# Three small loads moved behind the first gates, first rows ahead of the first block sum, first feature block turned in two banks

## The chip, the cores and the metric

The kernel runs on one core of one Trainium2 chip. The metric is the device time of one execution in microseconds (us); lower is better. Before the change the median of three runs is 175.96 us (175.79 to 176.62).

## The reference, cut to what matters

All data is f32. `x` is 2 batches x 512 rows x 512 features.

```
mod = (silu(c) @ wmod).reshape(2, 6, 1, 512)         # c: 2 x 512, wmod: 512 x 3072
sa, ca, ga, sb, cb, gb = mod[:, 0], ..., mod[:, 5]
ga, gb = guarded: sign(g) * max(|g|, 0.25)
h = layernorm(x) * (1 + ca) + sa
x = x + ga * (h @ (weight * block_mask).T)           # 32x32 blocks kept where the mask has any 1
h = layernorm(x) * (1 + cb) + sb
gate, up = (h @ Wg.T) * ag, (h @ Wu.T) * au          # 1376 inner features, ternary weights
x = x + gb * (((silu(gate) * up) @ Wd.T) * ad)
```

## The kernel before

Rows are cut into tiles of 128 (`TT` = 4 tiles a batch), features into blocks of 128 (`KT` = 4). Five instruction streams are written out by hand, one for each engine, in the order in which they run; semaphores alone tie them together. No scheduler moves anything.

SyncE (SP) issues the big loads in one long queue: the four `x` tiles of batch 0, the first mask block, the first modulation weights (`mod_ln1` 0, semaphore `d_ln1[0]`), the first attention weights, more modulation weights and masks, the `x` tiles of batch 1, and so on. After the first half of `mod_ln2` it waits for the normalised rows of batch 1 (`xn_ok`), issues seven moves of 32-row blocks inside SBUF (`move_first`, L246), then the rest of `mod_ln2` and the second `mod_gate` (L298 to L301), and then the chunks of the FFN weights (L308, L309).

ScalarE (ACT) issues four small loads first: `cond` (L385), the per-feature scales `scal` (L386), `adc` (L387) and the tail of `scal` (L389). The last three share the semaphore `d_small`, which is waited for by the first SiLU of the FFN (L504), by the first product behind it on VectorE (L698), and by `guard_gate(1)`.

The opening works as follows. VectorE (DVE) takes the statistics of the four tiles of batch 0 (`stats`), sums the first mask block (`sum_mask(0)`, L603) and normalises the first 256 features of the four tiles (`normalise_half(0, ...)`, L556). TensorE (PE) runs 17 warm-up matmuls (L1074), then `mask_blocks(0)` (L869: spreads the mask's block sums), `rows_first` (L813: the first modulation rows), the transposes of feature block 0 (`transposes(0, ...)`, L885), `columns(0)` (L859: turns the modulation rows), the transposes of feature block 1, and the first of the 32 attention products (`linear`, L906; two matmul records each). Between the attention products stand more of these small steps, in the table `between`. DVE turns the block sums into a 0/1 mask (`keep_blocks`, L608) and the rows into modulation columns (`mod_columns`, L615). GpSimd (POOL) multiplies the attention weights with that mask (`mask_weights`, L352). ACT copies the rows (`copy_rows`, L402) and applies scale and shift to the turned rows (`modulate`, L427 for the part that is done on its own, L430 for the rest).

Later steps that the prediction speaks of: `mask_blocks(2)` on PE lets DVE run `keep_blocks(2)` and then `normalise(1)` (L576), whose end lets SP issue its moves; `rows_last` on PE (48 instructions of L813) waits for the second `mod_gate`; after it stand the rest of the attention products and then the FFN (L935 gate and up products, L1005 down products, 22 steps). ACT checks each FFN weight chunk with `check_chunk` (L442) when the chunk has landed.

Of the kernel before, what the change touches and what calls it, by code (L numbers as in the profile page):

```python
# [26 lines left out]
ACT = mybir.ActivationFunctionType  # L27
# [3 lines left out]
P = 128  # L31
# [3 lines left out]
TT = 4  # L35
SEQ = TT * P
# [19 lines left out]
MOVES = [(i, j) for i in range(P // BLK) for j in range(P // BLK) if i != j]  # L56
BY_SYNC = 7
LAG = 2
FIRST_ALONE = [0, 3]
HELD = 4  # L60
HALF = D // 2
SHIFT = BLK + NB
# [14 lines left out]
def adaln_block(nc, x, att_w, att_mask, cond, mod_ln1, mod_ln2, mod_gate, w_gu, w_gu_tail, w_down,  # L77
                scales, scales_tail, down_scale, out):
    with ExitStack() as ctx:
# [3 lines left out]
        def sem(name):  # L83
            return ctx.enter_context(nc.semaphore(name))
# [116 lines left out]
        rstd_ok = sem("rstd_ok")  # L201
        xn_ok = sem("xn_ok")
        xt_done = sem("xt_done")
        h_first = sem("h_first")
        h_ok = sem("h_ok")
        h_hi = sem("h_hi")
# [176 lines left out]
        @block.scalar  # L383
        def _(act):
            act.dma_start(condt[:, :, :], cond).then_inc(d_cond, 16)  # L385
            act.dma_start(scal[:, 0:C - 1, :], scales).then_inc(d_small, 16)  # L386
            act.dma_start(adc[:, :], down_scale).then_inc(d_small, 16)  # L387
            act.wait_ge(zeroed, 2)
            act.dma_start(scal[0:FT, C - 1, :], scales_tail).then_inc(d_small, 16)  # L389
            act.wait_ge(d_cond, 16)  # L390
            act.wait_ge(zeroed, 3)
            act.activation(sc[:, :, :].rearrange("p j (i m) -> p j i m", m=SHIFT)[:, :, :, 0:NB],
# [3 lines left out]
            def copy_rows(n):  # L396
                act.wait_ge(rows_done, n + 1)
                if n == 0:
                    act.wait_ge(consts_ok, 6)
                if n == 3:  # L400
                    act.wait_ge(cols_done, 1)
                act.activation(rows[:, n % 3, :], bank[2 if n == 3 else 6][:, 0:P], ACT.Identity,  # L402
                               bias=onerow[:, 0:1]).then_inc(rows_copied, 1)
# [7 lines left out]
            def modulate(n):  # L411

                q, k = divmod(n, KT)
                layer, b = divmod(q, NB)
                act.wait_ge(xt_done, n + 1)
                act.wait_ge(modc_ok, SETS if layer else SET_OF[k] + 1)
                if q < 2:
                    dst = h1[:, b, k, :]
                else:
                    dst = hbuf[:, n % 2, :]  # L420
                    if n >= 10:
                        act.wait_ge(h_lo, n - 9)
                src = [bank[4 + n % 2][:, :], xturn[:, k, :], bank[n % 2][:, :], xn[:, k, :]][q]
                part = slice(0, SEQ)
                if n in FIRST_ALONE:
                    part = slice(P, SEQ)
                    act.activation(dst[:, 0:P], src[:, 0:P], ACT.Identity,  # L427
                                   bias=modc[:, layer, k, 2 + b:3 + b],
                                   scale=modc[:, layer, k, b:b + 1]).then_inc(h_first, 1)
                act.activation(dst[:, part], src[:, part], ACT.Identity,  # L430
                               bias=modc[:, layer, k, 2 + b:3 + b],
                               scale=modc[:, layer, k, b:b + 1]).then_inc(h_ok, 1)
# [19 lines left out]
            def round_d(s):  # L452
# [26 lines left out]
            act.wait_ge(d_line[0], 16 * GRP)  # L479
            act.dma_start(gates[:, 1, :], gate_line[0, 1].rearrange("k i -> (k i)").partition_broadcast(P))\  # L480
               .then_inc(d_gate_first, 16)
            copy_rows(3)
            check_chunk(next(check_at))
            check_chunk(next(check_at))
# [38 lines left out]
        def _(dve):  # L523
# [196 lines left out]
            for t in range(TT):  # L720
                stats(0, t)
            sum_mask(0)
            normalise_half(0, range(TT))
            keep_blocks(0)
            mod_columns(0)
            normalise_half(1, range(TT))
            sum_mask(1)
            stats(1, 0)
# [79 lines left out]
        def _(pe):  # L808
# [63 lines left out]
            def transposes(n, tiles=range(TT)):  # L872

                q, k = divmod(n, KT)
                dst = bank[4 + n % 2] if q == 0 else bank[n % 2]
                if k == 0:
                    pe.wait_ge(xn_ok, XN_FIRST + TT * q if q else TT)
                if n == 2:
                    pe.wait_ge(xn_ok, XN_FIRST)
                if q == 2 and k < 2:  # L880
                    pe.wait_ge(att_read, k + 1)
                elif n >= 2:
                    pe.wait_ge(h_ok, n - 1)
                for t in tiles:
                    last = pe.transpose(dst[:, t * P:(t + 1) * P], xn[:, t, k * P:(k + 1) * P],  # L885
                                        ident[:, :])
                if TT - 1 in tiles:
                    last.then_inc(xt_done, 1)

            def linear(b, k, t):  # L890

                alone = TT * b + k in FIRST_ALONE
                if t == 0 and alone:
                    pe.wait_ge(h_first, FIRST_ALONE.index(k) + 1)
                if t == (1 if alone else 0):
                    pe.wait_ge(h_ok, TT * b + k + 1)
                if t == 0:
                    if b == 0:
# [173 lines left out]
            pe.wait_ge(ident_ok, 1)  # L1072
            for _ in range(WARM_UP):
                pe.matmul(bank[0][:, 0:P], ident[:, :], ident[:, :], start=True, stop=True)  # L1074
            mask_blocks(0)
            rows_first()
            transposes(0, (0, 1))
            columns(0)
            transposes(0, (2, 3))
            transposes(1)  # L1080

            between = {
                (0, 0): [rows_second],
                (0, 1): [lambda: columns(1), lambda: mask_blocks(1)],
                (0, 2): [lambda: transposes(2)],
                (1, 1): [lambda: mask_blocks(2), lambda: transposes(3)],
# [94 lines left out]
```

## Time and profile before

| | |
|---|---|
| median of 3 runs | 175.96 us |
| the profiled execution's own time | 176.29 us |
| its span in the trace | 174.5 us |
| PE busy | 167.5 us (96%) |
| DVE busy | 102.6 us (59%) |
| ACT busy | 80.9 us (46%) |
| POOL busy | 27.7 us (16%) |
| granted PE clock | 0.999 of full speed |
| chain that ended last | PE 80%, DMA 8%, DVE 5%, SP's queue 4% |

The busy times are sums over an engine's instructions; matmuls are pipelined, so a busy PE is not a PE at its peak. The chain is followed back from the last instruction, at each step to what released it. Where the chain is on PE, only PE's own work or what it waits for can move the end; where it passes through DVE, SP's queue and a DMA, as it does up to 36.9 us, these set it.

### The profile page before, as it was taken

The numbers are of one execution on the slowest core, as the hardware profiler recorded it, in microseconds if no ns is written. First come the engines' busy times: TensorE is split into PE (matmuls) and PEld (weight loads), VectorE is DVE, ScalarE is ACT, GpSimd is POOL, SyncE is SP. The second block draws the span as 40 slices with busy tenths as digits, with TensorE's granted clock in tenths as the row PEclk, the third lists the DMA queues.
The fourth block names the chain that finished last, engine by engine and source line by source line (L and its number), as shares of the span: only waits on it lengthen the run. The fifth ranks groups of instructions, "written<-read, shape, count | busy, mean of one in ns | idle before, by whom it ended". The sixth has DMA issues, their size and how long they took to land.

```text
span 174.5 us, 2549 instructions
## 1 busy us (share of the span) xinstructions
PE 167.5 (96%) x892; PEld 128.4 (74%) x892; DVE 102.6 (59%) x216; ACT 80.9 (46%) x113; POOL 27.7 (16%) x32
## 2 busy tenths in 40 slices
PE   6889999979999999999999999999999999999992
PEld 6855554455468888888888888888888888888781
DVE  6778966990783999414855554437544313442574
ACT  3034005508999958755466442553425534252200
POOL 1233321930039310000000000007400000000000
PEclk9999999999999999999999999999999999999999
DMA  5999976999999501443000000001500000000014
GB/s 168 359 407 401 405 212 185 411 405 355 414 389 337 159 0 34 103 95 114 29 0 4 0 4 0 4 0 62 184 4 0 4 0 4 2 4 0 4 60 180
DMA packets 12789, 23.99 MB, mean 138 GB/s; under 512 B 3072, under 2 KB 5376, under 8 KB 12384
## 3 DMA queue, kind: packets, MB, share of 16 engines
q1 hardware_dynamic: 11056, 22.03, 35.1%
q10 hardware_dynamic: 1712, 1.66, 3.1%
q8 instruction: 16, 0.26, 0.6%
q14 instruction: 5, 0.04, 0.1%
HBM read 19.74 MB, written 2.11 MB: 125 GB/s over the span
## 4 chain that ended last, share of the span: by engine, by line
PE 80%; DMA 8%; DVE 5%; SPq 4%; issue 1%; ACT 0%; ACTq 0%
PE bank L935 46%; PE bank L1005 20%; PE bank L906 8%; DMA modw<-in_mod_gate 5%; DMA xt<-in_x 3%; SPq L246 3%; PE bank L813 2%; PE bank L991 2%; PE bank L885 2%; DVE wffn L576 1%; DVE xn L556 1%; DVE bns L542 1%; DVE xt L803 0%; SPq L263 0%; DVE xn L717 0%
## 5 line engine op out<-in xcount | busy, mean ns | idle before, releaser
L935 PE MATMUL bank<-ht,whi_gu 128*128 128x512 f32 x352 | 83.5, 391 | 0.0
L935 PEld LDWEIGHTS bank<-ht,whi_gu 128*128 128x128 f32 x352 | 65.6, 188 | 13.7 <-issue 0.5
L698 DVE SCALAR_TENSOR_TENSOR awork<-bank,scal,awork 128x512 f32<-128x512 f32 x22 | 16.5, 750 | 50.9 <-PE bank L935 47.6
L1005 PE MATMUL bank<-whi_dn,in_split 128*128 128x512 f32 x148 | 37.2, 391 | 0.0
L504 ACT ACTIVATE awork<-bank,scal 128x512 f32<-128x512 f32 x22 | 15.2, 689 | 45.3 <-PE bank L935 45.3
L1005 PEld LDWEIGHTS bank<-whi_dn,in_split 128*128 128x128 f32 x148 | 27.6, 188 | 6.0
L906 PE MATMUL bank<-awork,wffn 128*128 128x512 f32 x64 | 30.5, 603 | 0.2 <-ACT wffn L427 0.2
L449 ACT ACTIVATE whi_gu<-wffn 128x1024 fp32r<-128x1024 f32 x22 | 23.3, 1058 | 6.6 <-PE bank L935 6.6
L906 PEld LDWEIGHTS bank<-awork,wffn 128*128 128x128 f32 x64 | 11.0, 190 | 10.3 <-issue 9.0
L707 DVE TENSOR_TENSOR in_split<-awork,in_split 128x512 fp32r<-128x512 f32 x21 | 16.5, 785 | 0.7
L442 ACT ACTIVATE junk<-wffn 128x1536 uint8<-128x1536 uint16 x11 | 16.2, 1476 | 0.2
L379 POOL TENSOR_TENSOR xt<-xt,xn 128x512 f32<-128x512 f32 x4 | 5.2, 1346 | 54.5 <-DVE xn L717 54.5
L457 ACT ACTIVATE whi_dn<-wffn 128x512 fp32r<-128x512 f32 x21 | 13.1, 622 | 0.0
L542 DVE BATCH_NORM_STATS2 bns<-xt 128x6 f32<-128x512 f32 x16 | 10.8, 674 | 1.6 <-DMA xt<-in_x 1.5
L358 POOL TENSOR_TENSOR xt<-xt,xn 128x512 f32<-128x512 f32 x8 | 10.2, 1308 | 3.6 <-DVE xn L676 3.6
L402 ACT ACTIVATE rows<-bank,onerow 128x128 f32<-128x128 f32 x4 | 1.5, 368 | 19.9 <-PE bank L813 19.9
L705 DVE CAST in_split<-awork 128x512 fp32r<-128x512 f32 x21 | 9.0, 430 | 0.7
L345 POOL TENSOR_TENSOR rstd<-veps,mhalf 128x2 f32<-128x2 f32 x8 | 6.1, 763 | 15.2 <-DVE veps L547 15.1
L1074 PE MATMUL bank<-ident 128*128 128x128 f32 x34 | 6.6, 382 | 1.6 <-POOL ident L338 1.6
L1074 PEld LDWEIGHTS bank<-ident 128*128 128x128 f32 x34 | 6.4, 293 | 1.6 <-POOL ident L338 1.6
L813 PEld LDWEIGHTS bank<-modw,sc 128*32 128x32 f32 x192 | 5.0, 110 | 3.2 <-issue 3.2
L813 PE MATMUL bank<-modw,sc 128*32 128x128 f32 x192 | 6.1, 274 | 0.9 <-DMA modw<-in_mod_gate 0.9
(75 smaller groups left out, 109.6 us busy)
## 6 DMA issues: line engine op xcount, KB each, us to landing
wffn<-in_w_gu SPq DMA_DIRECT2D x10, 512.0 KB, 11.7
modw<-in_mod_ln SPq DMA_DIRECT2D x6, 512.0 KB, 7.1
wffn<-in_w_down SPq DMA_DIRECT2D x10, 256.0 KB, 13.1
xt<-in_x SPq DMA_DIRECT2D x8, 256.0 KB, 6.3
modw<-in_mod_gate SPq DMA_DIRECT2D x2, 1024.0 KB, 10.2
maskt<-in_att_mask SPq DMA_DIRECT2D x4, 256.0 KB, 8.0
awork<-in_att_w SPq DMA_DIRECT2D x4, 256.0 KB, 8.1
modw<-in_mod_ln SPq DMA_DIRECT2D x1, 1024.0 KB, 6.7
```

What stands on the lines that cost most here:

```text
L442: act.activation(junk[:, :], low, ACT.Copy, accum_out=chk[:, c:c + 1])\
L449: act.activation(whi_gu[:, s % 2, :], wffn[:, s % C, 0:2 * D], ACT.Copy)\
L457: act.activation(whi_d(s), raw_d(s % C), ACT.Copy).then_inc(wd_hi, 1)
L504: act.activation(silu_g[:, s % 2, :], bank[gu_bank(s, 0)][:, :], ACT.Silu, scale=scal[:, s % C, 0:1]).then_inc(silu_ok, 1)
L542: dve.bn_stats(bns[:, q, t, :], xt[:, n % (NB * TT), :]).then_inc(bn_done, 1)
L698: dve.scalar_tensor_tensor(inner[:, s % 2, :], bank[gu_bank(s, 1)][:, :], scal[:, c, 1:2], silu_g[:, s % 2, :], ALU.mult, ALU.mult).then_i ...
L707: dve.tensor_tensor(lo, inner[:, s % 2, :], hi.bitcast(F32), ALU.subtract)\
L813: last = pe.matmul(dst[BLK * j:BLK * (j + 1), 0:P], sc[:, j, at * BLK:(at + 1) * BLK], source(j), start=(i == 0), stop=(i == len(blocks) - 1))
L906: last = pe.matmul(bank[4 * b + t][:, :], h1[:, b, k, t * P:(t + 1) * P], awork[:, k, :], start=(k == 0), stop=(k == KT - 1))
L935: return pe.matmul(bank[gu_bank(s, u)][:, :], w, h, start=(k == 0 and part == 0), stop=(k == KT - 1 and part == 1))
L1005: last = pe.matmul(bank[4 + t][:, :], h, w, start=(c == 0 and part == 0), stop=(c == C - 1 and part == 1))
L1074: pe.matmul(bank[0][:, 0:P], ident[:, :], ident[:, :], start=True, stop=True)
```

## The change

1. ACT no longer issues the three `d_small` loads at the opening. It issues them behind the broadcast of the first gates (`gates[:, 1, :]`), just ahead of `copy_rows(3)`. ACT's wait for `zeroed` 2 goes (it waits for `zeroed` 3 right after).
2. DVE normalises only tiles 0 and 1 of the first 256 features before `keep_blocks(0)` and `mod_columns(0)`; tiles 2 and 3 follow behind them.
3. PE runs `rows_first` ahead of `mask_blocks(0)`. `transposes(0, (0, 1))` waits for two normalised tiles where it waited for four. `transposes(0, (2, 3))` waits for four and writes bank 3, where tiles 0 and 1 stay in bank 4; ACT's first `modulate` is cut at 256 columns (it was 128), and reads its second part from bank 3. `transposes(1)` stands behind the first attention product and no longer ahead of it.

PE, from the end of the warm-up. Here L869/L877 is `mask_blocks`, L813/L821 modulation rows, L885/L895 `transposes`, L859/L867 `columns`, L906/L918 the attention product (number before / after). First the kernel before:

```order
L869 MATMUL bank<-msum,blkones 128x16 [waits consts_ok,msum_ok]
L813 MATMUL bank<-modw,sc 32x128 [waits d_ln1_0,silu_c]
L813 MATMUL bank<-modw,sc 32x128 x7
L885 MATMUL bank<-ident,xn 128x128 [waits xn_ok]
L885 MATMUL bank<-ident,xn 128x128
L859 MATMUL bank<-ident,rows 128x128 [waits keep_ok,rows_copied]
L885 MATMUL bank<-ident,xn 128x128 [waits xn_ok]
L885 MATMUL bank<-ident,xn 128x128 x5
L906 MATMUL bank<-awork,wffn 128x512 [waits masked,h_first]
L813 MATMUL bank<-modw,sc 32x128 [waits rows_copied,d_ln1_2,d_ln1_1]
L813 MATMUL bank<-modw,sc 32x128 x15
L906 MATMUL bank<-awork,wffn 128x512 [waits h_ok]
```

The same place in the changed kernel:

```order
L821 MATMUL bank<-modw,sc 32x128 [waits d_ln1_0,silu_c]
L821 MATMUL bank<-modw,sc 32x128 x7
L877 MATMUL bank<-msum,blkones 128x16 [waits consts_ok,msum_ok]
L895 MATMUL bank<-ident,xn 128x128 [waits xn_ok]
L895 MATMUL bank<-ident,xn 128x128
L867 MATMUL bank<-ident,rows 128x128 [waits keep_ok,rows_copied]
L895 MATMUL bank<-ident,xn 128x128 [waits xn_ok]
L895 MATMUL bank<-ident,xn 128x128
L918 MATMUL bank<-awork,wffn 128x512 [waits masked,h_first]
L895 MATMUL bank<-ident,xn 128x128 x4
L821 MATMUL bank<-modw,sc 32x128 [waits rows_copied,d_ln1_2,d_ln1_1]
L821 MATMUL bank<-modw,sc 32x128 x15
```

The block sum has moved behind the rows, the wait on `xn_ok` ahead of the first product now covers two transposes (it covered six), and four transposes have moved from ahead of the first product to behind it.

DVE, from the first block sum. L603/L610 is `sum_mask`, L556/L563 `normalise_half`, L608/L615 `keep_blocks`, L615/L622 `mod_columns`. Before:

```order
L603 TENSOR_REDUCE msum<-maskt 128x16 [waits d_mask0]
L556 TENSOR_SCALAR xn<-xt,mv,rstd 128x256 [waits stats_ok,rstd_ok]
L556 TENSOR_SCALAR xn<-xt,mv,rstd 128x256
L556 TENSOR_SCALAR xn<-xt,mv,rstd 128x256 [waits stats_ok,rstd_ok]
L556 TENSOR_SCALAR xn<-xt,mv,rstd 128x256
L608 TENSOR_SCALAR keep<-bank 128x16 [waits blk_done]
L615 TENSOR_REDUCE modc<-bank 128x4 [waits cols_done]
L556 TENSOR_SCALAR xn<-xt,mv,rstd 128x256 x4
```

Changed:

```order
L610 TENSOR_REDUCE msum<-maskt 128x16 [waits d_mask0]
L563 TENSOR_SCALAR xn<-xt,mv,rstd 128x256 [waits stats_ok,rstd_ok]
L563 TENSOR_SCALAR xn<-xt,mv,rstd 128x256
L615 TENSOR_SCALAR keep<-bank 128x16 [waits blk_done]
L622 TENSOR_REDUCE modc<-bank 128x4 [waits cols_done]
L563 TENSOR_SCALAR xn<-xt,mv,rstd 128x256 [waits stats_ok,rstd_ok]
L563 TENSOR_SCALAR xn<-xt,mv,rstd 128x256 x5
```

Two of the four normalisations of the first half stand behind both waits on PE's results (`blk_done`, `cols_done`) now.

The diff:

```diff
--- before.py
+++ after.py
@@ -56,7 +56,7 @@
 MOVES = [(i, j) for i in range(P // BLK) for j in range(P // BLK) if i != j]
 BY_SYNC = 7
 LAG = 2
-FIRST_ALONE = [0, 3]
+FIRST_ALONE = {0: 2, 3: 1}
 HELD = 4
 HALF = D // 2
 SHIFT = BLK + NB
@@ -201,6 +201,7 @@
         rstd_ok = sem("rstd_ok")
         xn_ok = sem("xn_ok")
         xt_done = sem("xt_done")
+        first_turned = sem("first_turned")
         h_first = sem("h_first")
         h_ok = sem("h_ok")
         h_hi = sem("h_hi")
@@ -383,10 +384,6 @@
         @block.scalar
         def _(act):
             act.dma_start(condt[:, :, :], cond).then_inc(d_cond, 16)
-            act.dma_start(scal[:, 0:C - 1, :], scales).then_inc(d_small, 16)
-            act.dma_start(adc[:, :], down_scale).then_inc(d_small, 16)
-            act.wait_ge(zeroed, 2)
-            act.dma_start(scal[0:FT, C - 1, :], scales_tail).then_inc(d_small, 16)
             act.wait_ge(d_cond, 16)
             act.wait_ge(zeroed, 3)
             act.activation(sc[:, :, :].rearrange("p j (i m) -> p j i m", m=SHIFT)[:, :, :, 0:NB],
@@ -412,8 +409,9 @@
 
                 q, k = divmod(n, KT)
                 layer, b = divmod(q, NB)
-                act.wait_ge(xt_done, n + 1)
                 act.wait_ge(modc_ok, SETS if layer else SET_OF[k] + 1)
+                if n:
+                    act.wait_ge(xt_done, n + 1)
                 if q < 2:
                     dst = h1[:, b, k, :]
                 else:
@@ -423,10 +421,16 @@
                 src = [bank[4 + n % 2][:, :], xturn[:, k, :], bank[n % 2][:, :], xn[:, k, :]][q]
                 part = slice(0, SEQ)
                 if n in FIRST_ALONE:
-                    part = slice(P, SEQ)
-                    act.activation(dst[:, 0:P], src[:, 0:P], ACT.Identity,
+                    own = FIRST_ALONE[n] * P
+                    part = slice(own, SEQ)
+                    if n == 0:
+                        act.wait_ge(first_turned, 1)
+                    act.activation(dst[:, 0:own], src[:, 0:own], ACT.Identity,
                                    bias=modc[:, layer, k, 2 + b:3 + b],
                                    scale=modc[:, layer, k, b:b + 1]).then_inc(h_first, 1)
+                if n == 0:
+                    act.wait_ge(xt_done, 1)
+                    src = bank[3][:, :]
                 act.activation(dst[:, part], src[:, part], ACT.Identity,
                                bias=modc[:, layer, k, 2 + b:3 + b],
                                scale=modc[:, layer, k, b:b + 1]).then_inc(h_ok, 1)
@@ -479,6 +483,9 @@
             act.wait_ge(d_line[0], 16 * GRP)
             act.dma_start(gates[:, 1, :], gate_line[0, 1].rearrange("k i -> (k i)").partition_broadcast(P))\
                .then_inc(d_gate_first, 16)
+            act.dma_start(scal[:, 0:C - 1, :], scales).then_inc(d_small, 16)
+            act.dma_start(adc[:, :], down_scale).then_inc(d_small, 16)
+            act.dma_start(scal[0:FT, C - 1, :], scales_tail).then_inc(d_small, 16)
             copy_rows(3)
             check_chunk(next(check_at))
             check_chunk(next(check_at))
@@ -720,9 +727,10 @@
             for t in range(TT):
                 stats(0, t)
             sum_mask(0)
-            normalise_half(0, range(TT))
+            normalise_half(0, range(2))
             keep_blocks(0)
             mod_columns(0)
+            normalise_half(0, range(2, TT))
             normalise_half(1, range(TT))
             sum_mask(1)
             stats(1, 0)
@@ -874,25 +882,29 @@
                 q, k = divmod(n, KT)
                 dst = bank[4 + n % 2] if q == 0 else bank[n % 2]
                 if k == 0:
-                    pe.wait_ge(xn_ok, XN_FIRST + TT * q if q else TT)
+                    pe.wait_ge(xn_ok, XN_FIRST + TT * q if q else tiles[-1] + 1)
                 if n == 2:
                     pe.wait_ge(xn_ok, XN_FIRST)
                 if q == 2 and k < 2:
                     pe.wait_ge(att_read, k + 1)
                 elif n >= 2:
                     pe.wait_ge(h_ok, n - 1)
+                if n == 0 and tiles[0] == 2:
+                    dst = bank[3]
                 for t in tiles:
                     last = pe.transpose(dst[:, t * P:(t + 1) * P], xn[:, t, k * P:(k + 1) * P],
                                         ident[:, :])
+                if n == 0 and tiles[-1] == 1:
+                    last.then_inc(first_turned, 1)
                 if TT - 1 in tiles:
                     last.then_inc(xt_done, 1)
 
             def linear(b, k, t):
 
-                alone = TT * b + k in FIRST_ALONE
+                alone = FIRST_ALONE.get(TT * b + k, 0)
                 if t == 0 and alone:
-                    pe.wait_ge(h_first, FIRST_ALONE.index(k) + 1)
-                if t == (1 if alone else 0):
+                    pe.wait_ge(h_first, list(FIRST_ALONE).index(k) + 1)
+                if t == alone:
                     pe.wait_ge(h_ok, TT * b + k + 1)
                 if t == 0:
                     if b == 0:
@@ -1072,15 +1084,14 @@
             pe.wait_ge(ident_ok, 1)
             for _ in range(WARM_UP):
                 pe.matmul(bank[0][:, 0:P], ident[:, :], ident[:, :], start=True, stop=True)
+            rows_first()
             mask_blocks(0)
-            rows_first()
             transposes(0, (0, 1))
             columns(0)
             transposes(0, (2, 3))
-            transposes(1)
 
             between = {
-                (0, 0): [rows_second],
+                (0, 0): [lambda: transposes(1), rows_second],
                 (0, 1): [lambda: columns(1), lambda: mask_blocks(1)],
                 (0, 2): [lambda: transposes(2)],
                 (1, 1): [lambda: mask_blocks(2), lambda: transposes(3)],
```

## Rows read from the trace of the kernel before

**Rows 1.** the kernel by stretches: start:end, length, busy of PE, PEld, DVE, ACT, POOL

```profile
51.00:175.00 124.00, 120.17 (x551) 99.75 (x549) 64.48 (x117) 60.17 (x83) 12.97 (x11) 1.00 0.17 53
```

**Rows 2.** timeline of PE: start us, us, engine line op, idle before

```profile
36.91 2.83 PE L813 MATMUL bank<-modw,sc 128*32 128x128 f32 x96 [0.89 <-DMA modw<-in_mod_gate]
```

**Rows 3.** chain that ended last, 14 to 37 us: start us, us, what

```profile
18.93 0.14 PE bank L869 x2
...
21.91 0.62 SPq L246
...
22.57 0.82 SPq L246
...
25.46 0.59 SPq L246
...
27.86 8.81 DMA modw<-in_mod_gate
```

**Rows 4.** timeline of PE, 7 to 17 us

```profile
7.74 0.39 PE L1074 MATMUL bank<-ident 128*128 128x128 f32 x2
8.88 0.40 PE L869 MATMUL bank<-msum,blkones 128*128 128x16 f32 x2 [0.75 <-DVE msum L603]
9.20 0.65 PE L813 MATMUL bank<-modw,sc 128*32 128x128 f32 x16
...
10.44 0.27 PE L859 MATMUL bank<-ident,rows 128*128 128x128 f32 x1
...
11.54 1.12 PE L906 MATMUL bank<-awork,wffn 128*128 128x512 f32 x2 [0.17 <-ACT wffn L427]
...
15.76 0.60 PE L885 MATMUL bank<-ident,xn 128*128 128x128 f32 x4
16.19 2.74 PE L906 MATMUL bank<-awork,wffn 128*128 128x512 f32 x6
```

**Rows 5.** timeline of DVE, 8 to 15 us

```profile
8.74 1.38 DVE L556 TENSOR_SCALAR xn<-xt,mv,rstd 128x256 f32<-128x256 f32 x4
...
10.75 0.18 DVE L615 TENSOR_REDUCE modc<-bank 128x4 f32<-128x16 f32 x1 [0.56 <-PE bank L859]
...
14.22 0.69 DVE L542 BATCH_NORM_STATS2 bns<-xt 128x6 f32<-128x512 f32 x1 [0.68 <-DMA xt<-in_x]
```

**Rows 6.** timeline of POOL and ACT, 10 to 12 us

```profile
10.35 1.05 POOL L352 TENSOR_TENSOR awork<-awork,keep 128x512 f32<-128x512 f32 x1 [1.17 <-DVE keep L608]
...
11.03 0.46 ACT L427 ACTIVATE wffn<-bank,modc 128x128 f32<-128x128 f32 x1 [0.74 <-PE bank L885]
```

**Rows 7.** the load that rows_first waits for: ns, start us, landing

```profile
L269 SPq DMA_DIRECT2D modw<-in_mod_ln x1: 432/432/432, 3.1 to 3.1; - x1
...
DMA to landing us min/median/max: 5.9/5.9/5.9
```

**Rows 8.** DMA traffic, 2 to 6 us (whole, ACT's queue q10), then 8 to 12 us

```profile
DMA packets 1150, 1.14 MB, mean 286 GB/s; under 512 B 600, under 2 KB 600, under 8 KB 1150
...
q10 hardware_dynamic: 537, 0.02, 8.1%
...
DMA packets 625, 1.67 MB, mean 416 GB/s; under 512 B 71, under 2 KB 71, under 8 KB 625
```

**Rows 9.** timeline of ACT and its queue, 34 to 55 us

```profile
35.68 0.35 ACTq L480 DMA_DIRECT2D maskt<-gate_line  x1
39.80 0.37 ACT L402 ACTIVATE rows<-bank,onerow 128x128 f32<-128x128 f32 x1 [5.32 <-PE bank L813]
...
41.72 1.48 ACT L442 ACTIVATE junk<-wffn 128x1536 uint8<-128x1536 uint16 x1
...
54.17 0.68 ACT L504 ACTIVATE awork<-bank,scal 128x512 f32<-128x512 f32 x1
```

**Rows 10.** w_down load of FFN chunk 1: start us, landing

```profile
L309 SPq DMA_DIRECT2D wffn<-in_w_down x1: 442/442/442, 30.5 to 30.5; - x1
...
DMA to landing us min/median/max: 11.1/11.1/11.1
```

## The prediction

> **What bounds the kernel now.** I read the kernel by stretches first. From 51 us on PE is busy 120.17 of 124.00 us, with the end's last transfer among the rest, at full clock [rows 1]: that part is PE's own work, the change leaves it alone, and it can only be moved as a block. So the question is what sets its start. In the timeline of PE the last idle stretch of note stands ahead of `rows_last`: 0.89 us, until 36.91, ended by the DMA of the second `mod_gate` [rows 2]. PE was there at 36.02. From there back I followed the chain that ended last [rows 3]. The load is issued at 27.86 and takes 8.81 us; it is queued on SP behind seven block moves, the first of them at 21.91; these wait for `normalise(1)` on DVE, which follows at 19.1 to 19.2 on `mask_blocks(2)`, the PE piece that begins at 18.93 in the chain and ends at 19.07. Ahead of that PE works without a stop back to its first attention product at 11.54 [rows 4]. The first product is therefore the point to watch: each tenth by which PE reaches `mask_blocks(2)` later is a tenth later for SP, for the load and for the end; each tenth earlier is a tenth gained, as long as DVE keeps up. PE on its own has 0.89 us of slack at 36.02, so work added to PE behind `mask_blocks(2)` would cost nothing; here it is added ahead of it.
>
> **The move that costs: `transposes(1)`.** Four transposes go from ahead of the first product, where PE waited anyway, to behind it, where PE is the bound. Their price is the distance from the four transposes at 15.76 to the next product at 16.19: 0.43 us [rows 4]. From the first product to `mask_blocks(2)` PE issues the same instructions otherwise. So the change breaks even when the first product starts at 11.54 - 0.43 = 11.11.
>
> **When the first product can start.** Its waits are now two transposes behind four normalised tiles, `h_first`, and the masked weights. I build the chain from PE's first free moment.
> - `rows_first` stands first. PE's warm-up ends at 7.74 + 0.39 = 8.13 [rows 4]. The weights it waits for landed at 3.1 + 5.9 = 9.0 [rows 7]; if the opening loads gain a lead s from the removed small loads, 9.0 - s. In the kernel before, this landing was hidden behind the block sum (rows ran at 9.20); now nothing hides it. Start: the later of 8.13 and 9.0 - s.
> - `rows_first` 0.65, then `mask_blocks(0)` 0.32 (8.88 to 9.20) [rows 4]. `keep_blocks(0)` is as small as the reduction at 10.75, 0.18 [rows 5], plus 0.07 to hand over: 0.25. The block sum itself (DVE ends it at about 8.8) is no longer the last to come.
> - `columns(0)`: the matmul is 0.27 [rows 4], and I add about 0.09 on each side for handing over, an estimate: 0.45. The copy of the rows on ACT, 0.37 as in [rows 9], starts with the end of `rows_first` and runs beside the block sum and `keep_blocks`.
> - `mod_columns(0)` 0.18, then tiles 2 and 3 of the normalisation, 2 x 1.38/4 = 0.69 [rows 5]: 0.87. Tiles 0 and 1 ran in the wait for PE.
> - two transposes, half of 0.43, plus 0.05: 0.27.
>
> The sum behind the start of `rows_first` is 0.65 + 0.32 + 0.25 + 0.45 + 0.87 + 0.27 = 2.81. The two other waits are earlier: POOL's product, 1.05 [rows 6], from about 0.15 behind `keep_blocks`, is done 2.42 after that start, and ACT's first part (0.46 for 128 columns in [rows 6], about 0.55 for 256) 2.5 after it. DVE is the one that is late now, where the masked weights and ACT were late before (10.35 + 1.05 = 11.40, and 11.49).
>
> So the first product starts at max(8.13, 9.0 - s) + 2.81, and the end moves by that minus 11.11: by 0.70 - s, and not below -0.17, since the warm-up ends at 8.13. The second cut bank, the wider first part on ACT and the order on ACT cost nothing by themselves: the second part, some 0.55, is ready about a microsecond ahead of the third product, its first user.
>
> **How large is the lead s.** No row shows the opening without these loads, so I bound it. From below: ACT's queue took 8.1% of the 16 engines in 2 to 6 us, 0.32 us, with 537 packets [rows 8]. The three loads have 128, 128 and 96 rows, with a packet for each of 16 engines more, 400 of 544: 0.24 us. From above: in these four microseconds 1.14 MB moved, where 8 to 12 us moved 1.67 MB at 416 GB/s [rows 8]; if all of the missing 0.53 MB is theirs, 1.27 us. Less than nothing is excluded, since engines with fewer packets ahead don't land later. The upper end contains the start-up at 2 us and the share of `cond`, which stays (a quarter of the packets), so I take the middle, 0.75. The rate in 2 to 6 us is the nearest row, and 0.32 us of packet time doesn't explain 1.27 us of lost transfer.
>
> The end then moves by 0.70 - 0.75 = -0.05 us.
>
> The row shows 537 packets that together occupied the engines for 0.32 us [rows 8]. The Trainium skill (DMA: Bandwidth & Descriptors, Queues, rings and completion order) says that each DMA engine alternates between the queues that have work packet by packet. By that rule alone small packets cost the other queue only their own time: s is 0.24 and the end moves by +0.46. The same page (Specifications) says that a transfer under 512 B is handled by read-modify-write, below line rate, which points to more; the missing 0.53 MB agrees with the second. No run here shows either by itself yet.
>
> **DVE keeps up.** DVE waited 0.68 us for the first `x` tile of batch 1 at 14.22 [rows 5]; a lead on the loads shortens this wait, so DVE is ready no later than PE's `columns(1)`, and what it reads from PE sets it.
>
> **The small loads in their new place.** They are issued behind the gate broadcast at 35.68 + 0.35 [rows 9]; at 0.43 each, the price in [rows 7], ACT is through at 37.3, and needs to be at `copy_rows(3)` at 39.80 [rows 9]: 2.5 us of cover. They start behind the landing of `mod_gate` (27.86 + 8.81 = 36.67), so they don't delay it. Their data is wanted at 54.17 by the first SiLU [rows 9]. Behind ACT's three issues stand `copy_rows(3)` and the chunk checks. Cost: 0.
>
> **Sum.** The profiled execution took 176.29 us (its span 174.5 and 1.79 around it), 0.33 above the median of 175.96. It would become 176.24; against the median, 175.9 us. A measurement of this kernel can tell from no change about 0.5%, or 0.88 us; the forecast is far inside.
>
> **Rival 1: slower, `rows_first` holds everything.** If s is small, PE sits at `d_ln1[0]`, and with it `mask_blocks(0)`, `keep_blocks(0)`, both late normalisations and the first product. It decides from s = 0.70 down. With 0.24 the end moves by +0.46, 176.4 us; with none by +0.70, 176.7. For it: the landing at 9.0 against PE free at 8.13, and four more transposes. Against: the low rate of the opening.
>
> **Rival 2: slower, the small loads bite later.** `check_chunk(1)` starts at 41.72 [rows 9], and its chunk landed at 30.5 + 11.1 = 41.6 [rows 10]. There is 0.1 us of room. If the loads take 0.24 to 1.27 us of a stream that is full there too, check and then `modulate(8)` are late by up to 1.2 us. PE would pass on what its attention products don't cover: up to +0.9, 176.9. Against: ACT's work there has no user on PE until later.
>
> **Rival 3: faster, the lead is passed on whole.** The moves take 0.62 and 0.82 us at first and 0.59 later [rows 3]. If they are slow since older loads still fill the engines, a lead shortens them, and the load of `mod_gate` comes earlier than PE. Then PE's own readiness is the limit: -0.89 - 0.17 = -1.06, 174.9 us at the best; the excess of the two moves shown is only 0.26, and the later ones are no faster than 0.59 with the engines half empty, so 175.5 is more likely within this case.
>
> **Chances.** The forecast (no more than 0.4 either way) 0.64; rival 1 0.16; rival 2 0.08; rival 3 0.12. Its own range is 175.5 to 176.3. To hold 8 in 10 with the scatter of the runs (175.79 to 176.62), 175.2 to 176.8. Faster by over 0.5% needs nearly all of rival 3: 0.08. Slower by over 0.5% needs rivals 1 and 2 together or scatter: 0.09. Within 0.5%: 0.83.
>
> **What would show it.** In the trace of the changed kernel: the first `mod_ln1` landing (9.0 before, 8.25 forecast) and PE's `rows_first` directly behind it; the first product at about 11.06, with DVE's normalisation as its last releaser; the second product at about 13.55 (13.60 before by this sum); `normalise(1)` and the first move within 0.1 us of before; PE's idle time ahead of `rows_last` still ended by the DMA, near 0.9 us. The prediction fails if the landing is over 0.5 us away from 8.25 and the end follows it; if the first move starts earlier by over 0.3; or if ACT is late at `copy_rows(3)`.

## The result, and the profile after

The changed kernel takes 178.51 us (median; 177.20 to 178.98), the kernel before 175.91: a ratio of 1.0122 (95% interval 1.0092 to 1.0152). It is slower by 1.2% by that ratio, about 2.1 us; the two medians, of four runs each, lie 2.6 us apart, and in either reading the time is outside the range of 175.2 to 176.8. The profiled execution took 178.67 us, its span is 176.9 us: 2.4 above the span of before, and 1.8 outside the span as before. Its mean granted clock is 0.988, where before had 0.999. Of the four runs three have 0.988 (178.36 to 178.98) and one has 1.000; that one took 177.20. The ratios in this document leave out an execution more than 1.5% above the fastest of its kernel; numbers 2, 3 and 5 below have one each (180.53, 179.81 and 180.61 us).

The first products in the changed kernel's timeline of PE (start us, us, engine line op, idle before), which answers to [rows 4] and [rows 2]:

```profile
8.81 0.64 PE L821 MATMUL bank<-modw,sc 128*32 128x128 f32 x16 [1.36 <-DMA modw<-in_mod_ln]
...
11.71 0.44 PE L895 MATMUL bank<-ident,xn 128*128 128x128 f32 x2 [1.28 <-DVE xn L563]
11.99 1.67 PE L918 MATMUL bank<-awork,wffn 128*128 128x512 f32 x2
...
14.44 1.64 PE L821 MATMUL bank<-modw,sc 128*32 128x128 f32 x32
...
21.18 0.29 PE L877 MATMUL bank<-msum,blkones 128*128 128x16 f32 x2
...
39.28 2.83 PE L821 MATMUL bank<-modw,sc 128*32 128x128 f32 x96 [0.96 <-DMA modw<-in_mod_gate]
```

PE now stands still twice: 1.36 us for `rows_first`'s weights and 1.28 us for the late tiles. The first product starts at 11.99 (before 11.54, forecast 11.06) and takes 1.67 us instead of 1.12. `mask_blocks(2)` comes at 21.18 and `rows_last` at 39.28, 2.37 later than in [rows 2]: all of the loss is there by then, and what follows has the length it had. In the kernel before, `mask_blocks(2)` came 2.41 earlier:

```profile
18.77 0.29 PE L869 MATMUL bank<-msum,blkones 128*128 128x16 f32 x2
```

The same stretch by windows of the changed kernel (start:end, length, busy of PE, PEld, DVE, ACT, POOL, granted clock, DMA share, GB/s):

```profile
8.00:10.00 2.00, 1.19 (x20) 0.83 (x20) 0.92 (x4) 0.37 (x1) 0.03 (x1) 1.00 1.04 405
10.00:11.50 1.50, 0.34 (x2) 0.14 (x1) 1.02 (x3) 0.56 (x1) 1.05 (x1) 1.00 1.00 393
11.50:14.00 2.50, 2.29 (x7) 1.25 (x8) 2.10 (x7) 0.56 (x1) 0.00 (x0) 0.65 1.06 402
14.00:17.00 3.00, 3.00 (x38) 1.87 (x37) 0.83 (x2) 0.37 (x1) 0.00 (x0) 0.72 1.06 399
17.00:20.00 3.00, 3.00 (x14) 1.76 (x13) 2.61 (x8) 1.55 (x2) 1.74 (x2) 1.00 1.01 413
```

And of the kernel before:

```profile
10.00:11.50 1.50, 1.20 (x9) 0.97 (x9) 0.94 (x5) 0.76 (x3) 1.05 (x1) 1.00 1.01 400
11.50:14.00 2.50, 2.46 (x35) 1.41 (x36) 1.70 (x5) 0.81 (x2) 0.00 (x0) 1.00 1.06 395
14.00:17.00 3.00, 3.00 (x13) 1.62 (x12) 2.68 (x8) 1.49 (x3) 1.46 (x2) 1.00 1.05 393
```

The column of the granted clock falls to means of 0.65 over 2.5 us and 0.72 over 3.0 us. If PE ran either at full clock (2.4 GHz) or at half of it (1.2 GHz), that is some 3.4 us at half clock, and half of these, 1.7 us, is lost. Between 10.0 and 11.5 PE was busy 0.34 us of 1.5; before it was 1.20.

On DVE and POOL, the rows that answer to [rows 5] and [rows 6] (the same columns as the timeline):

```profile
9.82 0.17 DVE L615 TENSOR_SCALAR keep<-bank 128x16 f32<-128x16 f32 x1 [1.07 <-PE bank L877]
...
10.57 0.77 DVE L563 TENSOR_SCALAR xn<-xt,mv,rstd 128x256 f32<-128x256 f32 x1
...
11.26 0.40 DVE L563 TENSOR_SCALAR xn<-xt,mv,rstd 128x256 f32<-128x256 f32 x1
...
10.14 1.05 POOL L353 TENSOR_TENSOR awork<-awork,keep 128x512 f32<-128x512 f32 x1 [2.11 <-DVE keep L615]
```

The first late tile took 0.77 us, the second 0.40. The first started inside POOL's product (10.14 to 11.19) and ended 0.15 us behind it. The kernel before has such a tile too, inside the product of [rows 6] (10.35 to 11.40), and it ended 0.14 us behind that one:

```profile
10.84 0.70 DVE L556 TENSOR_SCALAR xn<-xt,mv,rstd 128x256 f32<-128x256 f32 x1
```

The chain on SP (start us, us, what), answering to [rows 3], keeps its lengths and is only later:

```profile
24.27 0.62 SPq L247
24.93 0.83 SPq L247
...
30.23 8.80 DMA modw<-in_mod_gate
```

### The profile page after: what moved, and what is told of

The parts are those of the page before. It is cut to its first block, busy times and chain, and to the rows that moved or that the text cites. A ratio compares the mean times of both kernels' runs of the same rounds, so it can differ in the third digit from the quotient of the medians.

```text
span 176.9 us, 2549 instructions
## 1 busy us (share of the span) xinstructions
PE 168.3 (95%) x892; PEld 128.6 (73%) x892; DVE 102.8 (58%) x216; ACT 81.1 (46%) x113; POOL 27.6 (16%) x32
## 4 chain that ended last, share of the span: by engine, by line
PE 81%; DMA 8%; SPq 4%; DVE 4%; issue 1%
PE bank L947 45%; PE bank L1017 20%; PE bank L918 9%; DMA modw<-in_mod_gate 5%; DMA modw<-in_mod_ln 3%; PE bank L821 3%; SPq L247 3%; PE bank L895 2%; PE bank L1003 2%; DVE wffn L583 1%; SPq L264 1%; DVE xn L563 1%; DVE xt L811 0%; DVE xn L724 0%; DVE xt L802 0%
## 5 line engine op out<-in xcount | busy, mean ns | idle before, releaser
L918 PE MATMUL bank<-awork,wffn 128*128 128x512 f32 x64 | 30.9, 612 | 0.0
L918 PEld LDWEIGHTS bank<-awork,wffn 128*128 128x128 f32 x64 | 11.0, 190 | 9.9 <-issue 9.1
L821 PE MATMUL bank<-modw,sc 128*32 128x128 f32 x192 | 6.6, 291 | 2.3 <-DMA modw<-in_mod_ln 1.4
L821 PEld LDWEIGHTS bank<-modw,sc 128*32 128x32 f32 x192 | 5.5, 118 | 4.4 <-issue 4.4
L895 PEld LDWEIGHTS bank<-ident,xn 128*128 128x128 f32 x32 | 4.3, 157 | 4.6 <-issue 2.9
L1086 PE MATMUL bank<-ident 128*128 128x128 f32 x34 | 5.9, 354 | 1.6 <-POOL ident L339 1.6
```

The source lines that it names most:

```text
L821: last = pe.matmul(dst[BLK * j:BLK * (j + 1), 0:P], sc[:, j, at * BLK:(at + 1) * BLK], source(j), start=(i == 0), stop=(i == len(blocks) - 1))
L918: last = pe.matmul(bank[4 * b + t][:, :], h1[:, b, k, t * P:(t + 1) * P], awork[:, k, :], start=(k == 0), stop=(k == KT - 1))
```

## The experiments

Times are medians. Ratios are to the kernel before in runs on the same chip, with their 95% intervals; its median over all of these runs is 176.2 us. Two theories stood at the start. Theory C: the granted clock falls because of PE's idle stretches in the opening, and costs most of the loss. Rival W: the waits alone do it. Theory P, on POOL's product beside the late tiles, came out of the trace later.

**1. Both idle stretches filled (e1_fill_both).** Matmuls of the warm-up's kind, with no reader.

```diff
-WARM_UP = 17
+WARM_UP = 23
+GAP_FILL = 5
...
             columns(0)
+            for _ in range(GAP_FILL):
+                pe.matmul(bank[0][:, 0:P], ident[:, :], ident[:, :], start=True, stop=True)
             transposes(0, (2, 3))
```

> The changed kernel with 6 more warm-up matmuls (23 instead of 17) and 5 matmuls of the same kind between columns(0) and transposes(0, (2, 3)); their results are not used. Theory C (the granted clock: PE idled 1.36 and 1.28 us in the opening, and then ran at half clock for 3.4 us): the clock stays at 1.00 through 8 to 20 us, the first product stays at about 12.0, and the time falls by some 1.7 us, to about 176.8. Rival W (the waits alone make it slower, and the clock is the same in any order): no change, 178.5.

Measured: 178.03 us, 1.0105 (1.0086 to 1.0125). All six runs have clock 1.00, as theory C said, but the time is not 176.8. Its PE timeline shows why for one execution, the slowest of the six (178.75):

```profile
6.63 3.24 PE L1087 MATMUL bank<-ident 128*128 128x128 f32 x23
9.80 0.65 PE L822 MATMUL bank<-modw,sc 128*32 128x128 f32 x16
...
12.98 1.02 PE L919 MATMUL bank<-awork,wffn 128*128 128x512 f32 x2
```

The warm-up, six matmuls longer, lasted until 9.8; `rows_first`, whose weights had landed at 3.1 + 4.7 = 7.8 in this execution, was held by it, and the first product came a microsecond later than in the changed kernel. The first product takes 1.02 us again. The experiment mixed a gain with a loss of my own making. How large this loss is in the other five runs isn't known: the same 23 matmuls end at 8.98 in the profile of number 2. A further 0.7 us of this one execution came later, where the load of `mod_gate` took 9.5 us where [rows 3] has 8.8.

**2. Only the longer warm-up (e2_fill_start).** The changed kernel with `WARM_UP = 23` alone.

> The changed kernel with only the 6 more warm-up matmuls. Theory C: if it takes both idle stretches for the clock to fall, 176.8 as with both filled; if the second (1.28 us, from 10.4 to 11.7) is enough, it stays at 178.5. Rival W: 178.5 in both.

Measured: 178.54 us, 1.0114 (1.0088 to 1.0140). Four of six runs show a clock of 0.98 to 0.99; the two with 1.00 took 177.57 and 177.76. In its profile (one of the four) the warm-up runs up to `rows_first`, and only the second stretch is left:

```profile
8.91 0.64 PE L822 MATMUL bank<-modw,sc 128*32 128x128 f32 x16
...
11.81 0.44 PE L896 MATMUL bank<-ident,xn 128*128 128x128 f32 x2 [1.28 <-DVE xn L564]
12.09 1.36 PE L919 MATMUL bank<-awork,wffn 128*128 128x512 f32 x2
```

So that one alone is enough for the clock to fall, though not each time.

**3. Only the second stretch filled (e9_fill_gap).** `WARM_UP = 17`, the five matmuls ahead of `transposes(0, (2, 3))`.

> The changed kernel with 5 matmuls of the warm-up's kind between columns(0) and transposes(0, (2, 3)), results not used, and the warm-up as it was. Theory C: this stretch of 1.28 us is what the clock falls for; the clock is 1.00 in all runs and the time that of the changed kernel's run at full clock, 177.2 (176.9 to 177.4). If the stretch ahead of rows_first counts as much, some runs still show 0.988 and 178.5.

Measured: 177.37 us (the median of seven), 1.0058 (1.0042 to 1.0075); six runs have clocks of 0.996 to 1.000, and the changed kernel's run at full clock took 177.20. The expected 1.00 in all runs was missed by one: the profiled execution took 179.81 us with a clock of 0.990. Its trace has full clock through the whole opening, though PE stood still for 1.64 us ahead of `rows_first`; the clock fell much later, behind another idle stretch, where the load of `mod_gate` took 9.84 us (8.81 in [rows 3]):

```profile
12.04 1.02 PE L919 MATMUL bank<-awork,wffn 128*128 128x512 f32 x2
...
19.61 0.29 PE L878 MATMUL bank<-msum,blkones 128*128 128x16 f32 x2
...
38.75 4.50 PE L822 MATMUL bank<-modw,sc 128*32 128x128 f32 x96 [1.99 <-DMA modw<-in_mod_gate]
```

`rows_last` took 4.50 us where it takes 2.83 at full clock. In the profile of number 7 PE stood still there for 1.96 us, and the clock stayed. So the filled stretch no longer costs clock in any of the seven, and the loss by the ratios is halved: theory C holds for half of it. What is left (0.6%, 1.0 us) is the order's.

**4. Only the loads moved (e3_loads_only).** The kernel before, with the three `dma_start` of `d_small` put ahead of `copy_rows(3)`.

> The kernel before with only the three small loads moved. Their lead shows by itself: the x tiles land about 1.5 us earlier (the fourth at 5.6 where it was 7.1) and the first mod_ln1 only 0.3 earlier, at 8.7. The first product may start 0.3 to 0.6 earlier, at 11.0 to 11.2, nothing else being added; then 175.4 to 175.6. If the earlier opening makes PE idle enough for the clock to fall, 177 or more.

Measured: 176.04 us, 1.0001 (0.9985 to 1.0017): no gain. In its profile the first `mod_ln1` landed at 3.1 + 5.4 = 8.5, the first product started at 10.99, `mask_blocks(2)` at 18.23 (18.77 before) and `rows_last` at 36.54 (36.91). The expected 175.4 to 175.6 were missed: over twelve runs no gain is left of it.

**5. Only the order changed (e4_order_only).** The changed kernel with the three loads back at the opening.

> The changed kernel with the three small loads back at the opening (parts 2 and 3 alone). The first mod_ln1 lands at 9.0 again; by the sum of the prediction the first product starts at 11.8 and the end moves by +0.7, 176.6 us, plus 1.7 if the clock falls here too (178.3).

Measured: 177.75 us, 1.0102 (1.0061 to 1.0144), as the whole change. Three runs show 0.996 to 1.000 (176.76, 176.95, 177.14), the others 0.98 to 0.99. The profiled one (176.76) is of the three at full clock, and PE stands still in it for the same 1.28 us ahead of the first product:

```profile
11.19 0.44 PE L896 MATMUL bank<-ident,xn 128*128 128x128 f32 x2 [1.28 <-DVE xn L564]
```

So the stretch doesn't always bring the clock down. In that profile the first `mod_ln1` landed earlier than in the kernel with the loads moved away, with the small loads at the opening:

```profile
DMA to landing us min/median/max: 5.1/5.1/5.1
```

That is 3.1 + 5.1 = 8.2, against 8.7 in the changed kernel. Over the fourteen profiles of this study the time from issue to landing is 5.1, 5.6, 5.9 and 6.0 us with the small loads at the opening (mean 5.65), and 4.7 to 5.8 in the ten with them moved (mean 5.5): it scatters from one execution to the next by more than they do to it. The order, parts 2 and 3, is the whole loss, as far as intervals of 0.3 to 0.4% to either side can tell.

**6. All four tiles ahead again (e12_four_tiles).**

```diff
-            normalise_half(0, range(2))
+            normalise_half(0, range(TT))
             keep_blocks(0)
             mod_columns(0)
-            normalise_half(0, range(2, TT))
```

> The changed kernel with all four tiles of the first half normalised ahead of keep_blocks(0) again (part 2 undone, parts 1 and 3 kept). Theory P (in the changed kernel the two late tiles run while POOL multiplies the first attention weights; the first of them took 0.77 us there, 0.36 for one of the two that ran ahead, and ends with POOL's product): here all four take 0.34 to 0.41 each ahead of POOL's product, the first product starts within 0.2 us of the end of that product, some 0.7 earlier than in the changed kernel, PE's long idle stretch ahead of transposes(0, (2, 3)) is gone, so the clock stays at 1.00, and the time is 176.1 to 176.5. Rival W (rows_first ahead of the block sum is the fault): no gain, 178.5.

Measured: 176.70 us, 1.0037 (1.0014 to 1.0060). PE and DVE in its timeline:

```profile
9.40 0.40 PE L876 MATMUL bank<-msum,blkones 128*128 128x16 f32 x2
...
11.35 1.10 PE L917 MATMUL bank<-awork,wffn 128*128 128x512 f32 x2 [0.68 <-ACT wffn L428]
...
8.29 1.37 DVE L563 TENSOR_SCALAR xn<-xt,mv,rstd 128x256 f32<-128x256 f32 x4
```

The block sum comes at 9.40, where the changed kernel has it at 9.39, and yet the first product starts 0.64 us earlier: the two late tiles are the difference. Two of twelve runs still show a clock of 0.99 (178.03, 178.13); 0.68 us of idle time ahead of the first product are left. The median is above the expected 176.1 to 176.5. What is left of the loss belongs to part 3 and to these two runs; the share of each isn't shown.

**7. The block sum ahead again (e11_sum_first).** As number 3, with `mask_blocks(0)` ahead of `rows_first()`.

> As the kernel with the second stretch filled, and mask_blocks(0) ahead of rows_first as in the kernel before. If the landing of the first mod_ln1 held the block sum, and with it keep_blocks, POOL and the late tiles: keep_blocks moves from 9.8 to about 8.9 and POOL's product ends at 10.3; columns(0) still waits for the rows (9.5 plus the copy), so mod_columns stays near 10.4, but the late tiles then run beside no product and take 0.36 each: first product at 11.3, 0.6 to 0.7 earlier, 176.5. If it is the late tiles alone: the same as the kernel with the second stretch filled, 177.2.

Measured: 176.79 us, 1.0030 (1.0011 to 1.0049) against 1.0058 in number 3. POOL's product ran from 9.26 to 10.31 and the late tiles from 10.24, nearly behind it; the first product started at 11.30:

```profile
9.26 1.05 POOL L354 TENSOR_TENSOR awork<-awork,keep 128x512 f32<-128x512 f32 x1 [0.76 <-DMA awork<-in_att_w]
...
11.30 1.02 PE L919 MATMUL bank<-awork,wffn 128*128 128x512 f32 x2
```

Number 3 has 12.04 for it; 0.2 us of the difference is `rows_first`, which started earlier in this execution. So either way to keep POOL's product off the late tiles gives about the same, as far as the intervals of numbers 6 and 7 tell.

**8. `transposes(1)` ahead again (e10_t1_ahead).** As number 3, with `transposes(1)` behind `transposes(0, (2, 3))`.

> As the kernel with the second stretch filled, and transposes(1) ahead of the first product again. By the prediction's sum four transposes are worth 0.43 us: 176.7 to 176.8 against 177.2, if ACT's first part and the masked weights are there before them; the first product itself then starts 0 to 0.4 later than with them behind it.

Measured: 177.33 us, 1.0067 (1.0047 to 1.0087): no different from number 3, and not the expected 176.7 to 176.8.

```profile
12.59 1.02 PE L919 MATMUL bank<-awork,wffn 128*128 128x512 f32 x2
...
19.73 0.29 PE L878 MATMUL bank<-msum,blkones 128*128 128x16 f32 x2
```

The first product starts at 12.59 instead of 12.04, and the four transposes are done by then. From it to `mask_blocks(2)` it is 7.14 us where number 3 has 7.57: the four transposes cost PE 0.43 us behind the first product, as the prediction said. But ahead of it they cost as much here. PE reaches them no earlier than the late tiles allow, so they can't hide there in this order.

**9. `transposes(1)` moved in the kernel before (e14_before_t1).**

```diff
             transposes(0, (2, 3))
-            transposes(1)
...
-                (0, 0): [rows_second],
+                (0, 0): [lambda: transposes(1), rows_second],
```

> The kernel before with transposes(1) alone moved behind the first product. If the step of the prediction holds, the first product starts where it did (it waits for the masked weights and for ACT), mask_blocks(2) comes 0.43 us later, and so does the end: 176.6, ratio 1.0025. PE then has another idle stretch of about 0.6 us ahead of the first product; if the clock falls for it, 178.

Measured: 176.37 us, 1.0018 (0.9995 to 1.0042). The expected 0.43 us would be 1.0025; the interval holds it, and holds nothing at all too. Two of twelve runs lost clock (177.93, 178.53). The profiled one is one of these:

```profile
11.15 1.99 PE L906 MATMUL bank<-awork,wffn 128*128 128x512 f32 x2 [0.60 <-ACT wffn L427]
```

```profile
11.50:14.00 2.50, 2.50 (x10) 1.03 (x13) 1.35 (x4) 0.15 (x1) 0.00 (x0) 0.50 1.05 394
```

The moved transposes had kept PE busy ahead of the first product. Without them it stands still for 0.60 us, and sometimes the clock falls. This execution also had 1.51 us of idle time ahead of its first block sum; number 4's profile has 1.30 us there and kept its clock, with 0.17 ahead of the first product.

**10. POOL's product held (e13_pool_waits).**

```diff
             inverse_deviation(0, 1)
+            pool.wait_ge(xn_ok, TT)
             mask_weights(0)
```

> The changed kernel, with POOL's first product of the attention weights held until all four tiles of the first half are normalised. Theory P (the late tiles are slow for POOL's product beside them): the first late tile takes 0.33 to 0.41 us where it took 0.77, both are done 0.4 us earlier from mod_columns on, and POOL's product then sets the first product, at about 12.4. Rival (a tile that follows a read of PSUM on DVE is slow by itself): 0.77 again.

Measured, one run and its profile: 177.55 us. DVE's late tiles and POOL:

```profile
10.36 0.73 DVE L564 TENSOR_SCALAR xn<-xt,mv,rstd 128x256 f32<-128x256 f32 x2
...
11.16 1.15 POOL L353 TENSOR_TENSOR awork<-awork,keep 128x512 f32<-128x512 f32 x1 [2.38 <-DVE xn L564]
...
12.46 1.10 PE L919 MATMUL bank<-awork,wffn 128*128 128x512 f32 x2 [0.88 <-POOL awork L353]
```

Both tiles together take 0.73 us with POOL out of the way; in the changed kernel they took 1.09 (10.57 to 11.66). Theory P holds in this execution, and the rival, that such a tile is slow by itself, falls. The product is late instead, as expected (12.46).

**11 and 12. One move given to ACT (e15_moves, e16_moves_loads).** The results pointed back to the chain of [rows 3], which bounds PE's last idle stretch; so I shortened it in the kernel before, in number 12 together with the moved loads.

```diff
-BY_SYNC = 7
+BY_SYNC = 6
...
             move_first(act, BY_SYNC + 4)
+            move_first(act, BY_SYNC + 5)
```

> The kernel before with one of SP's seven block moves given to ACT, behind its fifth (ACT waits for mod_columns there, from 25.1 to 26.2). SP reaches the loads ahead of rows_last 0.6 us earlier, and the end follows, as PE is ready 0.89 us ahead of that load: 175.5, ratio 0.9965. If the load's landing is set by the transfers and not by its issue, no change.

> The kernel before with that move on ACT and with the three small loads behind the first gates. If the small loads' place matters for the opening, 0.3 to 0.5 us better than the move alone, 175.1; if not, as the move alone.

Measured: the move alone 175.71 us, 0.9964 (0.9947 to 0.9981); with the loads moved too 175.61 us, 0.9976 (0.9959 to 0.9992). Both beat the kernel before, by 0.2 to 0.4%, and the loads add nothing. In number 11:

```profile
22.04 0.62 SPq L246
...
27.37 9.02 DMA modw<-in_mod_gate
```

```profile
36.63 2.83 PE L814 MATMUL bank<-modw,sc 128*32 128x128 f32 x96 [0.48 <-DMA modw<-in_mod_gate]
```

From the first move to the load of `mod_gate` it is 5.33 us where [rows 3] has 5.95, and PE's idle time ahead of `rows_last` falls from 0.89 to 0.48.

## Why the prediction was wrong

Two steps failed. "The end moves by that minus 11.11" took PE's way from there to `mask_blocks(2)` to run at full clock as before; for some 3.4 us of it the clock was halved, which cost 1.62 us, about two thirds of the loss in the profiled execution. And the start of the first product was off by 0.93 us, by the lead s and by the late tiles.

**What bounds the kernel** was read rightly: the loss at `mask_blocks(2)` (21.18 - 18.77 = 2.41 us) came out at `rows_last` as 2.37 and in the span as 2.4, through `normalise(1)`, SP's moves and the load, and numbers 11 and 12 gained on the same chain.

**The start of the first product** was forecast at 11.06 and came at 11.99. Of the 0.93, 0.56 is the later start of `rows_first` (8.81, forecast 8.25): 0.45 of it the lead s, 0.1 from the landing to PE, which the sum left out. The other 0.37 is the step "`mod_columns(0)` 0.18, then tiles 2 and 3 of the normalisation, 2 x 1.38/4 = 0.69". This second one is the step of the sum that failed by mechanism. I took the duration from a stretch where POOL ran only its small product for `rstd` (128x2, 8.31 to 9.18), beside which a tile took 0.41 us, and put the tiles into the 1.05 us of POOL's product, which I had in the same list. [rows 6] and the tile at 10.84 of the kernel before (0.70 us, also inside POOL's product, a row that I did not use) would have told it. The first tile took 0.77 instead of about 0.40, and number 10 shows that this is POOL's product. The Trainium skill (SBUF — State Buffer, Who interferes with whom) says that a `tensor_scalar` of VectorE can run in a mode with two ports and then contends with GpSimd for a shared pair of SBUF ports, which the one that issues first has for its whole instruction while the other is blocked. The traces agree: the tile that started 0.43 us into POOL's product took 0.77 us, the one that started 0.49 us into it took 0.70, and they ended 0.15 and 0.14 us behind it. They don't show in which mode the tiles ran.

**The lead s** was taken as 0.75. The first `mod_ln1` landed at 3.1 + 5.6 = 8.7, a lead of 0.3, and by numbers 4 and 5 even this need not be the small loads' doing. The bound from above gave them all of the missing 0.53 MB of [rows 8]. The four profiles with the small loads at the opening moved 1.13 to 1.21 MB from 2 to 6 us, the ten others 1.13 to 1.37, in the mean 0.11 more: a fifth of what I allowed them. The changed kernel moved 1.35 MB, and its `x` tiles landed up to 1.5 us earlier (the fourth at 2.1 + 3.5 against 2.1 + 5.0), but the load that counted did not: over all profiles the mean landing with the small loads away is 0.2 us earlier, inside the scatter and near the prediction's lower bound of 0.24. The prediction's 8.13 for the end of the warm-up was one execution's as well: the same 17 matmuls ended between 6.98 and 8.57 us in these profiles, at 7.44 in the changed kernel, which is why the stretch ahead of `rows_first` is as long as 1.36 us.

**`transposes(1)`** was priced rightly at 0.43: that is the difference between numbers 3 and 8 from the first product to `mask_blocks(2)`. As a time of the whole kernel number 9 gives 0.2% with an interval from nothing to 0.4%, which holds the price but does not show it. In the changed order moving it back gains nothing (number 8).

**The clock** is what the prediction left out: some two thirds of the loss in the profiled execution, and about half of it by the ratios. It said "at full clock" of the rest of the kernel and asked nowhere what the opening's idle time would do. The sum by the two mechanisms: the first product came 0.45 us later than before (11.99 - 11.54). From it to `mask_blocks(2)` it is 7.23 us before, 7.57 in the profiles of numbers 1, 3, 5 and 7, which kept full clock in that stretch, and 9.19 in the changed kernel. So order and waits cost 0.45 + 0.34 = 0.79 us and the clock 1.62, near the 1.7 that half of 3.4 us gives; together they are the 2.41. Filling the second stretch takes the ratio from 1.0122 to 1.0058 (number 3), and 177.37 is 1.1 us below the changed kernel's median. Why one run in four kept its clock stays open: number 5's profile has the same 1.28 us and full clock.

**Rival 1** was right in its mechanism: with the lead of 0.3 its own sum gives 0.70 - 0.3 = 0.4 us. Order and waits cost 0.8 us in the profile and 1.0 by number 3's ratio; about 0.4 of that are the late tiles beside POOL, which it hadn't priced. **Rival 2** did not come: ACT issued the three loads from 38.41 to 39.92 and was back 2.2 us ahead of `copy_rows(3)`, and from `rows_last` on the kernel has its old length:

```profile
39.44 0.48 ACTq L488 DMA_DIRECT2D scal<-in_scales_tail  x1
42.16 0.37 ACT L399 ACTIVATE rows<-bank,onerow 128x128 f32<-128x128 f32 x1 [5.32 <-PE bank L821]
```

**Rival 3**, a lead passed on, had no lead to pass on. The gain on its chain was there to be had in another way: one move less ahead of the load.

**The range** was too narrow on the slow side because all its cases lay on one clock.

## What to carry to other kernels

Before work is moved from an idle stretch of PE to a busy one, ask what is left in the stretch: what hides a wait can also keep the clock up, and an idle stretch can be paid for a second time behind it (here 1.28 us of it, then 1.62 us by the clock). Where VectorE and POOL overlap, a duration of a VectorE instruction is good for a place only with POOL in the same state; look what POOL does at the new place. And a landing read from one execution is a sample: let a change rest on it only when it holds over several.

## What the runs showed of the hardware

- Idle stretches of 1.36 and 1.28 us with some 1.6 us of work between them were followed by about 3.4 us at half clock in the profile, and three of the four runs have the same mean clock of 0.988. The second stretch alone brought it down in four of six runs (number 2); the first alone, 1.64 us, did not in number 3's profile. With 0.60 to 0.68 us ahead of the first product, and other idle time earlier in the opening, it fell in two of twelve runs each (numbers 6 and 9). In the kernel before, PE's stretches there were 0.75, 0.32 and 0.17 us, and none of its runs whose clock is listed fell below 0.996. Ahead of `rows_last` a stretch of 1.99 us was followed by a fall, one of 1.96 us was not (numbers 3 and 7).
- 128x256 f32 tensor_scalar on VectorE took 0.40 to 0.41 us alone and 0.70 to 0.77 when started inside a 1.05 us tensor_tensor of GpSimd; GpSimd's own took 1.15 us in number 10, where it was the later one.
- The first `mod_ln1` load, issued at 3.1 us each time, landed 4.7 to 6.0 us later over the fourteen profiles: 5.1 to 6.0 with the small loads at the opening, 4.7 to 5.8 without. The load of the second `mod_gate`, issued at 27 to 30 us, took 8.8 to 9.1 us in eleven of them and 9.5 to 9.8 in three (numbers 1, 3 and 7).
